# The spectral filter of a four-layer image network: three programs with barriers made one, loops written out, half of the inverse transform's input fetched early

## The reference

```python
H_full = h0 + H_cc                       # from numerators / denumerator, by FFT
X = jnp.fft.rfft2(x, s=(2 * l1, 2 * l2), axes=(-3, -2))
Y = jnp.einsum('...hwi,ijhw->...hwj', X, H_full)
y = jnp.fft.irfft2(Y, s=(2 * l1, 2 * l2), axes=(-3, -2))
return y[..., :l1, :l2, :]
```

## Time and profile before

| | us |
|---|---|
| median of three runs (lowest, highest) | 3954.57 (3943.47, 3962.06) |
| the profiled execution | 3962.51 |
| its span, from first to last instruction | 3960.7 |
| layer 0, spectrum to return | 797 to 1411 |
| layer 3, spectrum to return | 3350 to 3961 |

### The profile page before, as it was taken

The page is one execution under the profiler, slowest core; times in us unless marked ns, Lnnn a source line. Parts: engine busy times, 40 slices in busy tenths (PEclk is TensorE's granted clock), DMA queues, the critical chain, the costliest instruction groups (busy, mean ns, idle before and its releaser), DMA issues. The chain is left out here.

```text
span 3960.7 us, 94747 instructions
## 1 busy us (share of the span) xinstructions
PE 3515.7 (89%) x40648; PEld 2938.0 (74%) x40648; DVE 1510.6 (38%) x1831; ACT 1766.5 (45%) x1815; POOL 1519.8 (38%) x1130
## 2 busy tenths in 40 slices
PE   8999999849889769999798979999898977689887
PEld 8999999729888757777487767777477863489887
DVE  7666666231010133444543453444444444201001
ACT  2455544435554225555443445555444431445541
POOL 7666666216555213434143003333243000356540
PEclk9999999979999879999899989999999998899998
DMA  2344444477666451221122432112121443866665
GB/s 69 117 139 139 140 141 140 152 198 186 162 168 165 119 160 69 85 77 50 54 96 74 117 109 86 70 57 85 43 85 56 114 129 35 203 168 177 164 159 146
DMA packets 278472, 465.83 MB, mean 118 GB/s; under 512 B 36186, under 2 KB 115300, under 8 KB 276716
## 3 DMA queue, kind: packets, MB, share of 16 engines
q1 hardware_dynamic: 266332, 439.43, 39.5%
q10 hardware_dynamic: 11792, 21.12, 1.5%
HBM read 343.03 MB, written 114.29 MB: 115 GB/s over the span
## 5 line engine op out<-in xcount | busy, mean ns | idle before, releaser
L675 PE MATMUL c_acc<-c_shifted,c_filt 128*32 128x176 f32 (+8 forms) x16384 | 595.0, 302 | 122.1 <-issue 57.7
L675 PEld LDWEIGHTS c_acc<-c_shifted,c_filt 128*32 128x32 f32 x16384 | 567.5, 168 | 148.0 <-issue 133.8
L708 POOL TENSOR_TENSOR c_filt<-c_filt 64x2048 f32<-64x2048 f32 x64 | 350.3, 5474 | 686.8 <-DMA c_filt<-filters_dram 686.8
L242 PE MATMUL f_ab<-f_taps_ab,f_table 65*128 (+1 forms) x2080 | 299.4, 305 | 17.3 <-DMA f_table<-const_taps 7.0
L242 PEld LDWEIGHTS f_ab<-f_taps_ab,f_table 65*128 65x128 f32 x2080 | 280.5, 216 | 30.4 <-issue 22.2
L723 DVE TENSOR_TENSOR c_both<-c_acc,c_odd 128x256 f32<-128x256 f32 x64 | 31.0, 484 | 650.2 <-ACT c_odd L768 650.2
L1329 POOL TENSOR_TENSOR v_normed<-store,rstds 128x512 f32<-128x512 f32 x64 | 164.1, 2582 | 273.5 <-ACT v_affine L1348 181.0
L762 ACT ACTIVATE c_filt<-c_filt 64x1024 f32<-64x1024 f32 (+2 forms) x128 | 246.9, 1929 | 42.6 <-DMA c_filt<-filters_dram 34.6
L1178 POOL TENSOR_TENSOR sums<-sums,store 128x512 f32<-128x512 f32 x64 | 176.7, 2761 | 230.7 <-DVE store L1121 230.7
L763 ACT ACTIVATE c_filt<-c_filt 64x1024 f32<-64x1024 f32 (+2 forms) x128 | 244.9, 1913 | 0.0
L132 PE MATMUL q_acc_q<-xn,q_w_q 128*128 128x512 f32 x512 | 205.2, 401 | 39.6 <-DVE xn L127 39.6
(11 more groups left out here) (185 smaller groups left out, 8740.8 us busy)
## 6 DMA issues: line engine op xcount, KB each, us to landing
c_shifted<-spectrum_dram SPq DMA_DIRECT2D x256, 270.0 KB, 3.9
filters_dram<-f_stage SPq DMA_DIRECT2D x128, 512.0 KB, 4.1
c_filt<-filters_dram SPq DMA_DIRECT2D x256, 256.0 KB, 5.0
raw_weights<-in_L_conv_Wk SPq DMA_DIRECT2D x16, 2048.0 KB, 8.7
raw_weights<-in_L_conv_Wv SPq DMA_DIRECT2D x16, 2048.0 KB, 8.5
o_raw<-in_L_conv_Wout SPq DMA_DIRECT2D x128, 256.0 KB, 3.7
f_table<-const_taps SPq DMA_DIRECT2D x120, 260.0 KB
raw_weights<-in_L_conv_Wq SPq DMA_DIRECT2D x15, 2048.0 KB, 8.5
```

What stands on the lines that cost most here:

```text
L242: mm = nc.tensor.matmul(ab[blk % 2][:, k, part], table[:, blk % 2, k, part], taps_ab[:, q], start=True, stop=True)
L675: mm = nc.tensor.matmul(acc[k % 2][phase][32 * s:32 * s + 32, 0:B, LAGS * kb:HALF], filt[:, k, phase, :, :, 4 * kb + s].rearrange("p j c - ...
L708: nc.gpsimd.tensor_tensor(filt[0:64, k, SUM], filt[0:64, k, EVEN], filt[0:64, k, ODD], ALU.add).then_inc(filt_summed, 1)
```

## The change

The three programs become one, `global_filter`, with one set of buffers and no barrier inside. The PSUM banks are shared: the eight banks are turn, freq and tot first, then two sets of three accumulators, then five image buffers.

- Filters of the first three groups are loaded at the start, behind the image and the three tables, and inv_w behind them. PE's first wait is for all four tables (64 instead of 48).
- POOL's first three filter sums run during the spectrum. ACT's copies for groups 0 and 1 run before the square root in layer 0, and after the last spectrum rows in layer 3. DVE's clearing comes after its last scaling.
- SP waits for the spectrum's stores and loads rows at once. PE waits for rows, turned filters, the clearing and all `rows_ready`.
- All 32 groups are written out on all engines. The ring has three groups instead of four; group g+2 is loaded during group g.
- From group 16 on, SP also loads the even products of one output row (two DMAs of 128 KB a group) into the place of `cols`, after a wait for the first 16 groups' stores. The odd products are loaded after the last store into the place of `filt`, eight DMAs of 512 KB.
- At the return, PE does the even half of five units first (after all even products and group 30's output are there), then for each unit the odd half, a wait for DVE's add of that unit, and the even half of the unit five further on.
- ACT's order in a group is: copies for the next group, odd result, store.

```diff
+def global_filter(nc, layer, image, source, out_dram, spare, scratch, const, tag):
+    KB, RING = HALF // LAGS, 3
+    EARLY = 5
+        prod = [cols, filt[:].rearrange("p k h j c n -> p (k h j c n)")[:, 0:C * B * L].rearrange("p (j b h) -> p j b h", j=C, b=B)]
+        banks = [ps(f"bank{k}", [128, 4, L]) for k in range(8)]
+        turn, freq, tot = banks[0:4], banks[4:6], banks[6][:].rearrange("p b h -> p (b h)")[:, 0:64]
+        acc = [banks[0:3], banks[3:6]]
+        img = [banks[k] for k in (6, 7, 0, 1, 2)]
...
             sp.dma_start(fwd_w[:], const["fwd_w"]).then_inc(consts_in, 16)
+            for g in range(RING):
+                for q in range(4):
+                    load_filters(g, q)
+            sp.dma_start(inv_w[:], const["inv_w"]).then_inc(consts_in, 16)
...
+            for k in range(4):
+                sp.wait_ge(rows_stored[k], 16 * 2 * (2 * C // 4))
+            for g in range(2):
+                for m in range(4):
+                    load_rows(g, m)
+            for m in range(4):
+                sp.wait_ge(progress, SPREAD[2 * m + 1])
+                load_rows(2, m)
+            for g in range(1, GROUPS):
+                if g + 2 < GROUPS:
+                    for m in range(8):
+                        sp.wait_ge(progress, POINTS * g + SPREAD[m])
+                        if m < 4:
+                            load_filters(g + 2, m)
+                        else:
+                            load_rows(g + 2, m - 4)
+                if g >= GROUPS // 2:
+                    sp.wait_ge(progress, POINTS * g + 10)
+                    if g == GROUPS // 2:
+                        for k in range(RING):
+                            sp.wait_ge(stored[k], 16 * len(range(k, g, RING)))
+                    for c in range(2):
+                        load_products(0, c, slice(g - GROUPS // 2, g - GROUPS // 2 + 1), even_in)
+            for k in range(RING):
+                sp.wait_ge(stored[k], 16 * len(range(k, GROUPS, RING)))
+            for quarter in range(4):
+                for c in range(2):
+                    load_products(1, c, slice(4 * quarter, 4 * quarter + 4), odd_in[quarter])
...
+            if source is None:
+                act.wait_ge(var_ready, 1)
+            else:
+                lower_half(0)
+                lower_half(1)
+                act.wait_ge(var_ready, 1)
...
+            if source is None:
+                lower_half(0)
+                lower_half(1)
+            for g in range(GROUPS):
+                if 1 <= g < GROUPS - 1:
+                    lower_half(g + 1)
+                move_odd(g)
+                store(g)
...
+            pe.wait_ge(consts_in, 64)
...
+            for g in range(GROUPS):
+                group(g)
+
+            pe.wait_ge(even_in, 16 * 2 * C)
+            pe.wait_ge(acc_out, GROUPS - 1)
+            for u in range(EARLY):
+                back(u, 0)
             for u, (quarter, b) in enumerate(UNITS):
                 if b == 0:
-                    pe.wait_ge(prod_in[quarter], 16 * 4)
-                if u >= 4:
-                    pe.wait_ge(added, u - 3)
...
+                    pe.wait_ge(odd_in[quarter], 32)
+                back(u, 1).then_inc(done, 1)
+                if u + EARLY < len(UNITS):
+                    pe.wait_ge(added, u + 1)
+                    back(u + EARLY, 0)
```

More of the change, by code:

```diff
@@ L468, in _ @@
                 combine(2 * p + 1, 1)
-def spectrum(nc, image, source, scratch, const, tag):
+def global_filter(nc, layer, image, source, out_dram, spare, scratch, const, tag):
+    KB, RING = HALF // LAGS, 3
+    RUN = B * ROW - LAGS
+    POINTS, HALVES_DONE = 12, 8
+    SPREAD = (0, 1, 2, 4, 5, 6, 8, 9)
+    EVEN, ODD, SUM = range(3)
+    EARLY = 5
+    UNITS = [(quarter, b) for quarter in range(4) for b in range(B)]
     with ExitStack() as ctx:
@@ new lines, in global_filter, with acc_of @@
+        progress, odd_out, both_ready, acc_out = (sem(n) for n in ("progress", "odd_out", "both_ready", "acc_out"))
+        stored = [sem(f"stored{k}") for k in range(RING)]
+        even_in, odd_in = sem("even_in"), [sem(f"odd_in{k}") for k in range(4)]
+        done, added, out_stored = sem("done"), sem("added"), sem("out_stored")
+        block = ctx.enter_context(nc.Block())
+        def acc_of(g, phase):
+            return acc[g % 2][phase][:].rearrange("p b h -> p (b h)")[:, 0:B * HALF].rearrange("p (b h) -> p b h", b=B)
@@ new lines, in drain, with finish @@
+            def drain(g):
+                dve.wait_ge(odd_out, g + 1)
+                nc.vector.tensor_tensor(both[:, g % 2], acc_of(g, EVEN), odd[:, g % 2, :, 1:], ALU.add).then_inc(both_ready, 1)
+                if g >= RING:
+                    dve.wait_ge(stored[g % RING], 16 * (g // RING))
+                nc.vector.tensor_tensor(out[:, g % RING, :, :, 0], acc_of(g, EVEN), odd[:, g % 2, :, 0:HALF], ALU.add)
+            def finish(g):
+                dve.wait_ge(progress, POINTS * (g + 1))
+                dve.wait_ge(both_ready, g + 1)
+                nc.vector.tensor_tensor(out[:, g % RING, :, :, 1], acc_of(g, SUM), both[:, g % 2], ALU.subtract).then_inc(acc_out, 1)
@@ L571, in turn_channel, with product, group, back @@
                 mm.then_inc(turn_ready, 1)
-            pe.wait_ge(consts_in, 48)
+            def product(g, phase):
+                k = g % RING
+                for kb in range(KB):
+                    for s in range(4):
+                        moving = total[:, k, B * s:B * s + B] if phase == SUM else shifted[:, k, s, :, phase]
+                        mm = nc.tensor.matmul(
+                            acc_of(g, phase)[32 * s:32 * s + 32, :, LAGS * kb:HALF],
+                            filt[:, k, phase, :, :, 4 * kb + s].rearrange("p j c -> p (j c)"),
+                            moving[:, :, 0:HALF - LAGS * kb], start=kb == 0, stop=kb == KB - 1)
+                    if kb % 4 == 3:
+                        mm.then_inc(progress, 1)
+            def group(g):
+                pe.wait_ge(rows_in[g % RING], landed(g))
+                pe.wait_ge(turned, 2 * g + 1)
+                if g == 0:
+                    pe.wait_ge(cleared, 2)
+                    pe.wait_ge(rows_ready, 2 * C)
+                if g >= 2:
+                    pe.wait_ge(acc_out, g - 1)
+                product(g, EVEN)
+                product(g, ODD)
+                pe.wait_ge(turned, 2 * g + 2)
+                pe.wait_ge(rows_summed, g + 1)
+                product(g, SUM)
+            def back(u, par):
+                quarter, b = UNITS[u]
+                for j in range(4):
+                    mm = nc.tensor.matmul(img[u % EARLY][:, j], prod[par][:, 4 * quarter + j, b], inv_w[:, par],
+                                          start=par == 0 and j == 0, stop=par == 1 and j == 3)
+                return mm
+            pe.wait_ge(consts_in, 64)
             if source is not None:
@@ L1636, in build @@
         local_conv(nc, io, image, scratch, const, "l_")
[L1637 removed]
         with nc.sbuf_tensor("spare", [128, 2, 8, 512], F32) as spare:
[L1639 to L1640 removed]
+            global_filter(nc, 1, image, None, out, spare, scratch, const, "g3_")
 def patch_mixer(nc, io, half, mean, rstd, raw, scratch, const):
```

323 lines of the change are left out of this document (95 added, 228 removed).

## The result

The changed kernel takes 3895.22 us, the median of four runs (3891.75 to 3900.45); beside it the kernel before took 3958.32 (3943.47 to 3962.17). The ratio is 0.9849, with a 95% interval of 0.9818 to 0.9879: 1.5% faster. The profiled execution took 3891.88 us; its span is 70.6 us shorter than that of before.

A forecast was written before the change was run, and what follows sets the result against it. PE's lag convolution was taken to lose time to loop jumps and to loads beside it, with PE idle around it. +27 - 28 - 52 - 12 = -65 from the median 3954.6 gave 3890 us, range 3850 to 3948.

The forecast's parts named there:

- A: Start of spectrum: PE's first turn waits for inv_w behind 12 filter loads; +14.8 us layer 0, +12.4 layer 3, sum +27.
- B: Spectrum to first product: barrier, filter loads, sums and copies go or have run before; -28 us, bounds -18 to -32.
- C: Convolution groups written out: no jump, straight groups at 13.78 us; 444.7 instead of 472.3 and 469.0, sum -52.
- D: Return: even products fetched early, even halves of five units first; -7.4 us, layer 3 -4.7, sum -12.
- 3.15 MB take 14.2, inv_w 0.6: Start of spectrum: time in us for the filter loads at 222 GB/s, then inv_w, together +14.8 on PE's first turn.
- Rival 1: Start of spectrum: inv_w isn't held up by the filter loads; +12 instead of +27, 3875 us; chance 0.12.
- the jump costs 4.9 us a batch: Looped convolution: a four-group batch ended by a jump takes 60.0 us, four straight groups of 13.78 would take 55.1.
- filters landed before POOL looks for them: Sign expected within the written-out groups: filters land at 9.6 us, before POOL's 5.5 us sum.
- rival 3: Return: PE's waits of 0.9 in every 2.7 us lower its clock, units' matmuls double; 49 us in all, 3939; chance 0.07.
- Rival 2: Convolution: loads are the bound, groups stay at 14.7 us without the jump; -13, 3942; chance 0.08.
- Rival 4: Convolution: written-out code starves PE for instructions, 1.8 us more a group; +39, 3994; chance 0.10.
- Rival 5: Convolution: straight code hides the instruction fetch entirely, groups at 12.3 us; -152, 3803; chance 0.03.

The follow-up runs named there:

- e3: Changed kernel with inv_w on a semaphore of its own, which PE waits for only before the return: 3887.07 us, single run.
- e1: Kernel before with only the loops of convolve written out, on all engines; ring of four and three programs kept: 3889.90 us, ratio 0.984.
- e11: Kernel before with PE's loop over eight groups a pass instead of four, 4 jumps instead of 12: 3918.15 us, single run.
- e8: Changed kernel without the filter loads from group 3 on, old filters used again: 3824.57 us, single run.
- e7: Changed kernel with inv_w on its own semaphore, ACT's copies after the last rows, and the return's even half one unit later: 3846.02 us, ratio 0.9744.
- e4: Changed kernel with inv_w on its own semaphore and ACT's copies for groups 0 and 1 after the last spectrum rows in both layers: 3877.68 us, ratio 0.9796.
- e9: Changed kernel without the row loads from group 3 on, old rows used again: 3848.24 us, single run.

## Why the prediction was right

3890 was forecast and 3895 measured, inside the range of the likeliest case. From profile to profile it was -65 against -70.6. The terms, however, were off in both directions, by 18, 9.5 and 4 us, and that the sum is off by only 5 is in part luck:

| us, both layers | forecast | measured |
|---|---|---|
| A, later start of the spectrum | +27 | +31.2 |
| spectrum itself | 0 | -2.7 |
| B, spectrum to first product | -28 | -25.6 |
| C, groups written out | -52 | -70.0 |
| D, return | -12 | -2.5 |
| sum | -65 | -69.6 |

**A** held in mechanism. From the start of the program, layer 0's first turn moved from 13.0 to 29.9 us, layer 3's matmul for the mean from 10.7 to 25.0. The term mis-sized is "3.15 MB take 14.2, inv_w 0.6": inv_w landed 16.9 us later in the program than fwd_w had. Rival 1, inv_w getting past the filters, is refuted: PE's first turn is released by it in both layers. e3 shows what that wait costs.

**B** held: 8.6 and 8.7 us from the end of the last store's issue to the first product, 21.4 and 21.5 before. The first rows took longer than the 3.9 that I put in.

**C** was mis-sized by 18. The 28 groups were put at 388.3 us a layer and took 380.7 and 382.7. The step "the jump costs 4.9 us a batch", with the 13.78 behind it, is the largest part of it. It was worked out by comparing a pass with its own straight groups at 13.78, but these groups are slower within a loop than written out: 13.5 and 13.3 in e1, which keeps the old ring and the old programs. By e11 and e1 a jump costs 6.1 to 6.7 us in all, 1.2 to 1.8 more than I had, 14 to 22 over twelve. "31.8 for groups 0 and 1" was also too much (28.5 and 29.4). Against it stands the fetch of even products, put at 2.5 a layer and found at some 5. Its direction and its kind, a slowing in proportion to more bytes, held. PE had no wait within the groups but "issue". One sign of C, "filters landed before POOL looks for them", did not come: each of POOL's 64 sums stood until its filters had landed (519.3 us in all, in the page above). It cost PE nothing.

**D** was wrong in layer 3. "DVE's last add 46 after the last product" was 47.8 in layer 0, with units of 2.83 where I had 2.7, so that layer gave -4.9. In layer 3 it became +2.4 instead of -4.7. This is rival 3 in small, the low clock at the return: three units took 4.56, clock 0.84 over the return against 0.97 in layer 0. The rival had the doubled matmuls right and the extent wrong, three units of one layer and not all of both. Its cause, the waits in every unit, is not shown.

Rival 2, groups bound by their loads, fell with e1 and with the changed kernel itself: the groups left 14.7. Rival 4, PE starving in straight code, is real in kind and refuted in its size. Its mechanism, late instruction packets, makes most of the 1.3 us a group over 12.3, with stops at 67 of 168 places, which the 13.78 of the forecast already held; 1.8 us more a group did not come. Rival 5, 12.3 a group, is what e8 shows with the filter loads gone. So the rule behind it holds on this chip, under a condition that this kernel doesn't meet.

The forecast also let the reader believe that the fusion pays (A, B and D together -13). By e1 it doesn't: starts and returns together are even (+0.4), and the early fetch takes 10 from the convolutions. A and D were self-made waits, and e7 takes both away.

## What to carry to other kernels

Write out a loop around some thousand PE instructions before anything else is fused: a jump costs PE its standstill and then a slower start, here 6 to 7 us, and one engine's edit was the whole gain. When programs are merged, look at each wait that the merging lets grow: a table that is needed last but counted with the first, copies put in front of a short step that all depend on, a bank reused in the very next step. And read a stage from its own borders, since errors in four terms can cancel to a total that looks understood.

## What the runs showed of the hardware

**DVE waits for POOL.** In e3 the statistics of layer 3 come earlier and meet POOL's filter sums at another point. The timeline of e3, then the same DVE instruction of the changed kernel:

```profile
3329.19 4.50 POOL L608 TENSOR_TENSOR g_filt<-g_filt 64x2048 f32<-64x2048 f32 x1 [106.62 <-DMA g_filt<-filters_dram]
...
3331.03 2.75 DVE L662 TENSOR_TENSOR g_dev<-g_stats,g_mean 128x64 f32<-128x64 f32 x1
```

```profile
3334.22 0.24 DVE L661 TENSOR_TENSOR g_dev<-g_stats,g_mean 128x64 f32<-128x64 f32 x1
```

64 columns take 2.75 us instead of 0.24, and end when POOL's sum does (3329.19 + 4.50 = 3333.69, with the DVE end at 3333.78). In e4 it is 3.16. In the changed kernel POOL was running a sum from 3329.73 to 3334.26, whose end the DVE instruction at 3334.22 just met. The Trainium skill (SBUF — State Buffer, Who interferes with whom) says that a DVE instruction with two inputs in SBUF contends with a GpSimd one that reads it, and that the later one blocks for the whole of the other. The trace agrees to 0.1 us. A copy shows it as well, DVE's clearing copy of layer 0, beside POOL in the kernel before and alone in the changed one:

```profile
879.36 2.35 POOL L711 TENSOR_TENSOR raw_weights<-c_shifted 128x1024 f32<-128x1024 f32 x1
879.51 2.90 DVE L738 COPY c_filt<-c_filt 64x768 f32<-64x768 f32 x1 [12.50 <-POOL c_filt L708]
```

```profile
867.39 0.86 DVE L631 COPY g_filt<-g_filt 64x768 f32<-64x768 f32 x1
```

**A small table behind large loads waits for them.** inv_w's issue at 811.35 landed at 827.97, behind 12 loads of 256 KB into 64 partitions.

**Instruction packets come late beside other transfers.** One packet of 16 KB answers to 256 matmul and weight-load records. PE's stops in straight code all stand at that distance from each other or at multiples of it: 67 in 56 groups with all loads, 28 without the row loads (e9), 4 without the filter loads (e8).

**A clock that halves in one of two like places.** The two returns run the same instructions with the same gaps of 0.8 us. In layer 3 the granted clock was 0.50 from 3839.5 to 3853.1 and three units took 4.56 us; in layer 0 it was 0.50 for 3.4 us only, before the first add. In the other returns with these gaps one unit or none was slow, so the gaps alone don't decide it.
